# Attention partials summed and divided in the feed-forward stage, a third PSUM bank for turned quarters, and negated scores

## The chip, the cores and the metric

One Trainium2 chip, and one of its cores. The metric is the device time of one execution in microseconds (us); lower is better.

## The reference, cut to what matters

One transformer block over `x` of 2 batches, 2048 tokens and 512 features, with 16 heads of 32 features, in float32:

```python
q = (x @ Wq + bq)...; k = (x @ Wk + bk)...; v = (x @ Wv + bv)...     # x: layer norm, scaled and shifted
scores = jnp.einsum('bhqd,bhkd->bhqk', q / math.sqrt(HEAD_DIM), k) + attention_bias   # (2, 16, 2048, 2048)
scores = jnp.where(src_mask, -jnp.inf, scores)
probs = jax.nn.softmax(scores, axis=-1)
ctx = jnp.einsum('bhqk,bhkd->bhqd', probs, v)         # back to (2, 2048, 512)
x = x + (ctx @ Wo + bo)
h = _ln(x) * g2 + beta2
x = x + gelu2(h @ W1 + b1) @ W2 + b2                  # 2048 hidden features
# then pairs of features are rotated by theta and phi
```

The attention bias alone is 512 MB, and it is read once.

## The kernel before, in words

The kernel has three stages, one after the other: `phase_a` (layer norm, q, k and v, written to DRAM; the mask is turned into a bf16 penalty), `phase_b` (attention) and `phase_c` (output projection, feed-forward and rotation). Data go from stage to stage through DRAM scratch tensors.

**Stage B.** A tile is 128 queries of one head against all 2048 keys. There are 512 tiles, in 64 trips of 8 (`R = 8`). A trip is one head and 1024 queries; it has two units (`hh`) of 4 tiles. The tiles live in `ring`, which has 8 slots of 128x2048 float32, one for each `j` of a trip. Every engine runs its own list of steps, one step for each tile, and waits on semaphores that the others count up:

- SyncE loads the bias of a tile into its slot as soon as the tile that had the slot eight steps before has been turned (`sp.wait_ge(turned, ...)`). Behind the load of `j == 0` stand four loads of the next trip's keys, behind those of `j == 2` and `j == 6` four loads of queries. On the first of 16 trips of a group the penalty (`penb`, 512 KB a tile) is loaded too.
- GpSimd adds the penalty (L450).
- TensorE computes scores in two halves of 1024 (`score`, L601). VectorE adds each half to the slot and keeps a running maximum (`add`, L506), and then makes `neg_max` out of it (L520).
- ScalarE takes the exponential of a tile and its sum (L555).
- TensorE turns (transposes) the tile in four quarters of 512 through two PSUM banks (`turn`, L618). ScalarE copies quarters 0 and 1 to `probT` (L564), VectorE quarters 2 and 3 (`copy_quarter`, L492).
- TensorE multiplies with the values (`weigh`, L634), in four bands of 32 partitions, each of which holds a partial context. For each unit ScalarE copies the four bands out (`ctxp`, L571). TensorE adds them up with eight matmuls against `sel4` (`close`, L646), VectorE takes the reciprocal of the sums (L524) and multiplies by it (`ctx_out`, L532), and ScalarE stores 64 KB to `ctx_scratch`.

In a step `i` VectorE runs: add of half 0, add of half 1, `neg_max`, quarter 2 and quarter 3 of tile `i-2`. TensorE runs: scores of tile `i`, quarters 0 and 1 of tile `i-2`, `close` (at `j % 4 == 2`), `weigh`, quarters 2 and 3.

**Stage C.** 8 units of 512 tokens. The feed-forward of unit `u` (`ffn`) and the front of unit `u+1` (`front`: context turned, Wo, layer norm, turned) are interleaved in 18 steps `f` by the helper `supertiles`:

```python
for f in range(FB): front(0, f)
with eng.Fori(0, NU - 1) as u:
    for f in range(FB + 2):
        ffn(u, f)
        if f < FB:
            front(u + 1, f)
```

`ffn` at step `f` is, on TensorE, the up matmuls of block `f` (L944) and the down matmuls of block `f-2` (L954); on ScalarE the gate (L812); on VectorE `hidden` (L872). At step 17 VectorE adds the residual and rotates (L877 to L890), and GpSimd adds the two halves of the rotation (L781). `front` at steps 0 to 3 turns one quarter of the context of the next unit: TensorE transposes `ctx_in` (L916) and ScalarE copies it out to `ctxT` (L799). VectorE adds `bo` to `xm_in` at step 0 (L832).

Of the kernel before, what the change touches and what calls it, by code (L numbers as in the profile page):

```python
# [18 lines left out]
F32 = mybir.dt.float32  # L19
# [20 lines left out]
MASKED = -3.0e38  # L40
QSCALE = 1.0 / math.sqrt(DH)
# [24 lines left out]
def phase_a(nc, sem, x, timestep, mask, theta, phi, W_ada, b_ada, Wq, bq, Wk, bk, Wv, bv, freqs,  # L66
            q_parts, k_parts, v_heads, xm_scratch, pen_scratch, ident, sel4, trig):

    with ExitStack() as ctx:
# [76 lines left out]
        def _(pool):  # L146

            nc.gpsimd.memset(ident[:], 0.0).then_inc(const_ready, 1)
            nc.gpsimd.memset(sel4[:], 0.0).then_inc(const_ready, 1)
            pool.wait_ge(const_ready, 2)  # L150
            nc.gpsimd.affine_select(out=ident[:], in_=ident[:], compare_op=ALU.not_equal, fill=1.0,
                                    base=0, pattern=[[-1, P]], channel_multiplier=1).then_inc(const_ready, 1)
            for j in range(4):
                pool.wait_ge(const_ready, 3 + j)
                nc.gpsimd.affine_select(out=sel4[:], in_=sel4[:], compare_op=ALU.not_equal, fill=1.0,
                                        base=-DH * j, pattern=[[-1, DH]], channel_multiplier=1).then_inc(const_ready, 1)
# [159 lines left out]
        def _(pe):  # L316
# [11 lines left out]
            pe.wait_ge(const_ready, 7)  # L328
# [22 lines left out]
def phase_b(nc, sem, side, q_parts, k_parts, v_heads, pen_scratch, ctx_scratch, ident, sel4):  # L351
# [4 lines left out]
    R = 8  # L356
# [5 lines left out]
    TRIPS = GROUPS * H  # L362
    NT = TRIPS * R
    UNITS = TRIPS * 2
    assert R == 2 * QT and QR * P == N
    with ExitStack() as ctx:
# [9 lines left out]
        max_part = sb("max_part", [P, R, CH])  # L376
        neg_max = sb("neg_max", [P, R])
        sums = sb("sums", [P, R])
        recip = sb("recip", [P, 2, QT])
        ctxp = sb("ctxp", [P, TOK])  # L380
        ctx_out = sb("ctx_out", [P, 2, QT, DH])
        scores = [ctx.enter_context(nc.psum_tensor(f"scores{i}", [P, CW], F32)) for i in range(CH)]
        bankT = [ctx.enter_context(nc.psum_tensor(f"b_T{i}", [P, N], F32)) for i in range(2)]
        bank_ctx = ctx.enter_context(nc.psum_tensor("bank_ctx", [P, TOK], F32))
        bank_sum = ctx.enter_context(nc.psum_tensor("bank_sum", [P, TOK], F32))
# [9 lines left out]
        max_ready = sem("max_ready")  # L395
# [6 lines left out]
        ctx_summed = sem("ctx_summed")  # L402
        recip_ready = sem("recip_ready")
        ctx_normed = sem("ctx_normed")
        ctx_stored = [sem(f"ctx_stored{i}") for i in range(2)]
# [3 lines left out]
        block = ctx.enter_context(nc.Block())  # L409

        @block.sync
        def _(sp):
# [27 lines left out]
            for i in range(2):  # L440
                sp.wait_ge(ctx_stored[i], 16 + TRIPS * 16)
# [36 lines left out]

        @block.vector
        def _(dve):  # L480
            dve.sem_inc(ctx_normed, 1)

            def copy_quarter(it, j, n):

                t, k = it * R + j - 2, (j - 2) % R
# [523 lines left out]
```

## Time and profile before

| | |
|---|---|
| median of three runs | 3857.47 us (3857.29 to 3860.09) |
| the profiled execution | 3858.61 us |
| its span, first to last instruction | 3857.0 us |
| mean granted TensorE clock | 0.965 |
| busy: PE, DVE, ACT, POOL | 93%, 66%, 49%, 56% of the span |
| stage B, from the first GpSimd tile to the first load of stage C | 519.4 to 2721.4 us |
| stage C | 2721.4 us to the end |

The profiled execution takes 1.6 us more than its span. PE stands for TensorE matmuls, PEld for its weight loads, DVE for VectorE, ACT for ScalarE, POOL for GpSimd, SP for SyncE; SPq and ACTq are the DMA issues of these engines. Ends of matmuls are modelled and overlap, so that starts are the better guide to TensorE's pace.

### The profile page before, as it was taken

The page shows a single profiled execution, that of the slowest core. Times are in us where ns is not written, and L with a number is a line of the kernel's source. Part 1 is how long each engine was busy: PE and PEld are TensorE (multiplying, and loading weights), DVE is VectorE, ACT ScalarE, POOL GpSimd, SP SyncE. Part 2 cuts the span into 40 slices and gives each one's busy share as a digit, 9 for nine tenths or more (in the row PEclk, how much of TensorE's full clock was granted, in tenths as well). Part 3 has the DMA queues.
Part 4 walks back from the last instruction along what each step waited for, and adds up shares of the span by engine and source line. Part 5 has one row for each costly group of instructions (what it writes and reads, how often), then busy time and mean ns, then how long its engine had stood idle before and what let it go on. Part 6 is the DMA issues. An engine that isn't in the chain of part 4 may idle for free. (4 is left out here: it accounts for less than half of the span.)

```text
span 3857.0 us, 64984 instructions
## 1 busy us (share of the span) xinstructions
PE 3589.8 (93%) x18848; PEld 2074.9 (54%) x18848; DVE 2561.2 (66%) x4882; ACT 1899.6 (49%) x2483; POOL 2165.7 (56%) x595
## 2 busy tenths in 40 slices
PE   6778769999999999999999999999699999999997
PEld 2334336666666666666666666666344444444443
DVE  3444449999989999899999899999322323232232
ACT  1221227777777777777777777777211111111110
POOL 0000059999989999999999999999000000000000
PEclk8889879999999999999999999999799999999999
DMA  5556489999999999999999999997511101101000
GB/s 188 169 173 201 147 288 319 315 313 312 319 348 317 316 312 312 337 331 313 317 315 313 341 319 314 317 313 271 155 22 33 22 11 33 22 22 22 11 11 11
DMA packets 327444, 822.20 MB, mean 213 GB/s; under 512 B 165376, under 2 KB 181760, under 8 KB 250624
## 3 DMA queue, kind: packets, MB, share of 16 engines
q1 hardware_dynamic: 277376, 746.44, 57.6%
q10 hardware_dynamic: 45312, 58.74, 5.6%
q0 software_dynamic: 4736, 16.78, 1.2%
q8 instruction: 10, 0.16, 0.0%
q14 instruction: 10, 0.08, 0.0%
HBM read 737.95 MB, written 83.89 MB: 213 GB/s over the span
## 5 line engine op out<-in xcount | busy, mean ns | idle before, releaser
L450 POOL TENSOR_TENSOR ring<-ring,penb 128x2048 f32<-128x2048 f32 x512 | 2089.4, 4119 | 599.6 <-DMA penb<-pen_scratch 542.5
L555 ACT ACTIVATE ring<-ring,neg_max 128x2048 f32<-128x2048 f32 x512 | 1029.1, 2010 | 515.4 <-DVE neg_max L520 515.4
L618 PEld LDWEIGHTS b_T<-ident,ring 128*128 128x128 f32 x8192 | 886.7, 141 | 623.5 <-ACT probT L564 427.6
L618 PE MATMUL b_T<-ident,ring 128*128 128x128 f32 x8192 | 1158.7, 281 | 1.9 <-DVE probT L492 1.3
L492 DVE COPY probT<-b_T 128x512 f32<-128x512 f32 x1024 | 668.0, 684 | 70.5 <-PE b_T L618 70.5
L506 DVE CUSTOM_DVE_ANT_0 ring<-scores,ring,max_part 128x1024 f32<-128x1024 f32 x512 | 657.6, 1284 | 74.2
L506 DVE CUSTOM_DVE_ANT_0 ring<-scores,ring 128x1024 f32<-128x1024 f32 x512 | 622.2, 1215 | 43.6 <-PE scores L601 43.6
L601 PE MATMUL scores<-keys,queries 128*128 (+1 forms) x2048 | 606.5, 418 | 46.6 <-DMA queries<-q_parts 45.4
L781 POOL TENSOR_TENSOR y_out<-rot_a,rot_b 128x512 f32<-128x512 f32 x32 | 50.3, 1572 | 1020.8 <-DVE rot_b L890 1020.0
L564 ACT COPY probT<-b_T 128x512 f32<-128x512 f32 x1024 | 542.8, 580 | 30.2 <-PE b_T L618 24.0
L634 PE MATMUL bank_ctx<-probT,values 128*32 128x512 f32 x4096 | 546.8, 607 | 0.0
L944 PE MATMUL c_up<-hT,w 128*128 (+1 forms) x1024 | 478.3, 611 | 41.6 <-DVE hidden L872 40.7
L954 PE MATMUL c_acc<-w,hidden 128*128 128x512 f32 x1024 | 458.9, 592 | 0.0
L872 DVE SCALAR_TENSOR_TENSOR hidden<-c_up,b_col,gate 128x512 f32<-128x512 f32 x128 | 95.9, 750 | 519.1 <-ACT gate L812 517.7
L812 ACT ACTIVATE gate<-c_up,b_scaled 128x512 f32<-128x512 f32 x128 | 88.0, 687 | 673.2 <-PE c_up L944 673.0
L601 PEld LDWEIGHTS scores<-keys,queries 128*128 128x128 f32 x2048 | 349.3, 191 | 96.8 <-issue 45.7
L944 PEld LDWEIGHTS c_up<-hT,w 128*128 128x128 f32 x1024 | 197.2, 197 | 275.1 <-issue 232.1
L954 PEld LDWEIGHTS c_acc<-w,hidden 128*128 128x128 f32 x1024 | 194.0, 190 | 241.8 <-issue 241.5
L221 ACT ACTIVATE std<-mean_var,eps_a 128x4 f32<-128x4 f32 x8 | 2.4, 297 | 311.8 <-DVE mean_var L283 311.8
L837 DVE TENSOR_TENSOR x<-c_fore,xm_in 128x512 f32 (+1 forms) x32 | 22.1, 692 | 167.5 <-PE c_fore L925 167.5
L646 PE MATMUL bank_sum<-sel,ctxp 128*128 128x32 f32 x1024 | 125.1, 266 | 0.7 <-ACT ctxp L571 0.7
L646 PEld LDWEIGHTS bank_sum<-sel,ctxp 128*128 128x128 f32 x1024 | 124.4, 192 | 1.6 <-ACT ctxp L571 1.6
(91 smaller groups left out, 1926.1 us busy)
## 6 DMA issues: line engine op xcount, KB each, us to landing
ring<-in_fside_Bx16xSxS SPq DMA_DIRECT2D x512, 1024.0 KB, 5.8
keys<-k_parts SPq DMA_DIRECT2D x256, 256.0 KB, 6.8
values<-v_heads ACTq DMA_DIRECT2D x128, 256.0 KB, 6.0
queries<-q_parts SPq DMA_DIRECT2D x512, 64.0 KB, 6.8
pen_scratch<-pen SPq DMA_DIRECT2D x8, 2048.0 KB, 7.2
penb<-pen_scratch SPq DMA_DIRECT2D x32, 512.0 KB, 12.3
xin<-in_x ACTq DMA_DIRECT2D x8, 1024.0 KB, 5.2
mask_in<-in_mask_Bx1xSxS_bk ACTq DMA_DIRECT2D x8, 1024.0 KB, 7.3
```

The costliest lines, as they stand in the source:

```text
L450: nc.gpsimd.tensor_tensor(ring[:, j, :], ring[:, j, :], penb[:, j, :], ALU.add).then_inc(masked, 1)
L492: nc.vector.tensor_copy(probT[:, hh, QR * n:QR * (n + 1), q * P:(q + 1) * P], bankT[n - 2][:].rearrange("p (c q) -> p c q", c=QR)).then_in ...
L506: nc.vector.tensor_tensor_reduce(out=at, in0=scores[c][:], in1=at, scale=1.0, scalar=max_part[:, j, c - 1:c] if c else MASKED, op0=ALU.add ...
L555: nc.scalar.activation(ring[:, k, :], ring[:, k, :], ACT.Exp, bias=neg_max[:, k:k + 1], accum_out=sums[:, k:k + 1]).then_inc(exp_done, 1)
L564: nc.scalar.copy(probT[:, hh, QR * n:QR * (n + 1), q * P:(q + 1) * P], bankT[n][:].rearrange("p (c q) -> p c q", c=QR)).then_inc(out_act, 1)
L601: last = nc.tensor.matmul(scores[c][:, n * N:(n + 1) * N], queries[:, hh, q * P:(q + 1) * P], keys[:, bass.ds(it % 2, 1), c * CW + n * N:c ...
L618: last = nc.tensor.transpose(bankT[n % 2][:, c * P:(c + 1) * P], ring[:, slot, at:at + P], ident[:])
L634: last = nc.tensor.matmul(bank_ctx[DH * c:DH * (c + 1), :], values[:, hh, QR * n + c, :], probT[:, hh, QR * n + c, :], start=(n == 0), sto ...
L646: last = nc.tensor.matmul(bank_sum[:, t * DH:(t + 1) * DH], ctxp[:, t * P:(t + 1) * P], sel4[:], start=True, stop=True)
L872: nc.vector.scalar_tensor_tensor(out=hidden[:, f % 4, :], in0=up[f % 2][:], scalar=b1_col[:, f:f + 1], in1=gate[:, f % 2, :], op0=ALU.add, ...
L944: last = nc.tensor.matmul(up[f % 2][:], w1[:, c, f * P:(f + 1) * P], hT[:, bass.ds(u % 2, 1), c, :].rearrange("p o n -> p (o n)"), start=( ...
L954: last = nc.tensor.matmul(acc[t][:], hidden[:, k % 4, t * P:(t + 1) * P], w2[:, k, :], start=(k == 0), stop=(k == FB - 1))
```

## The change

- `close`, `sel4`, the bank `bank_sum`, the reciprocal and the multiplication leave stage B. ScalarE stores `ctxp` itself, all four bands, 256 KB a unit. It waits for the store of the unit before it copies again.
- The freed bank becomes a third bank for turned quarters. Waits that stood ahead of a group of matmuls now stand inside the group before (ahead of its last part). VectorE's copy of quarter 3 moves from the end of step `i` to between the two adds of step `i+1`.
- The adds write the negated score and keep a running minimum. That minimum is the bias of the exponential, so `neg_max` is gone. Minima and sums of all tiles are kept on chip for stage C (one copy of 128x8 a trip).
- In stage C the sixteen 256 KB loads of partial contexts of a unit (in four groups `c`, two buffers) replace four loads of 256 KB. VectorE takes the reciprocals and adds a term from the minima at step 0, spreads four heads' reciprocals over 32 columns each (`recip_wide`), and TensorE transposes these in place of the context. VectorE adds up the four bands (`tensor_reduce` over 4x512) and multiplies by the turned reciprocals. ScalarE no longer copies `ctxT`. `bo` is added at step 3.

```diff
         def turn_bank(t, n):
+            return bankT[(0, 1, 2, 0)[n] if t % 2 == 0 else (2, 1, 0, 2)[n]]
...
             def step(it, j):                                   # VectorE, stage B
                 add(it, j, 0)
+                keep_low(it, j)
+                copy_quarter(it, j, 3, 3)
                 add(it, j, 1)
-                if live(i, NT):
-                    dve.wait_ge(added, i * CH + CH)
-                    nc.vector.tensor_scalar(neg_max[:, j:j + 1], max_part[:, j, CH - 1:CH], -2.0, 0.5, ALU.mult, ALU.mult).then_inc(max_ready, 1)
-                copy_quarter(it, j, 2)
-                if dividing:
-                    dve.wait_ge(exp_done, i - 1)
-                    nc.vector.reciprocal(recip[:, hh, :], sums[:, hh * QT:(hh + 1) * QT]).then_inc(recip_ready, 1)
-                copy_quarter(it, j, 3)
-                if j % QT == 2: ...   nc.vector.tensor_tensor(ctx_out[:, hh, :, :], bank_sum..., recip..., ALU.mult)
+                copy_quarter(it, j, 2, 2)
...
+            def free_before_turn(it, j, c):                    # TensorE, ahead of the last matmul of a score half
+                t = it * R + j - 2
+                if live(t, NT):
+                    if c == 0:
+                        pe.wait_ge(exp_done, t + 1)
+                    else:
+                        need(pe, out_dve, t * 2 - 1)
...
+                for c in range(4):                             # weigh
+                    if c == 2 and live(t, NT):
+                        need(pe, out_dve, t * 2)
...
-                if j % QT == 2:
-                    close(it, j)
...
+                if j % QT == 1 and live(unit, UNITS):          # ScalarE
+                    act.wait_ge(pv_done, PV0 + unit + 1)
+                    act.wait_ge(ctx_stored, unit * 16 + 16)
+                    nc.scalar.copy(ctxp[:], bank_ctx[:]).then_inc(ctx_copied, 1)
...
             def load(v):                                       # SyncE, stage C
+                for c in range(DB):
+                    if isinstance(v, int) and c == 2:
+                        load_vectors()
+                    need(sp, parts_used, v * DB + c - 1)
+                    for k in range(4):
+                        sp.dma_start(parts[DH * k:DH * (k + 1), c % 2, :, :],
+                                     ctx_scratch[bass.ds(v * H + 4 * c + k, 1)].rearrange("o (g d) q -> d (o g) q", d=DH)).then_inc(part_ld[c % 2], 16)
...
                 if f == 0:                                     # VectorE, stage C, front(v, f)
+                    nc.vector.tensor_scalar(undefined[:], in_unit(low_all, v), 2.0, 0.0, ALU.mult, ALU.mult)
+                    link(nc.vector.reciprocal(recip[:], in_unit(sums_all, v)), 1)
+                    link(nc.vector.tensor_tensor(recip[:], recip[:], undefined[:], ALU.add), 2)
+                    need(dve, wo_done, v * QT)
+                if f < DB:
+                    need(dve, recip_turned, v * DB + f - 1)
+                    nc.vector.tensor_copy(recip_wide[:, f % 2]..., recip[:, 4 * f:4 * f + 4, :]...to_broadcast([P, QT, 4, DH])).then_inc(wide_ready, 1)
+                    dve.wait_ge(part_ld[f % 2], v * 128 + (f // 2) * 64 + 64)
+                    nc.vector.tensor_reduce(ctxT[:, f, :], parts[:, f % 2].rearrange("p g q -> p q g"), AXIS_X, ALU.add).then_inc(parts_used, 1)
+                    dve.wait_ge(parts_used, v * DB + f + 1)
+                    dve.wait_ge(recip_turned, v * DB + f + 1)
+                    nc.vector.tensor_tensor(ctxT[:, f, :], fore[f % 2][:], ctxT[:, f, :], ALU.mult).then_inc(ctxT_ready, 1)
...
                 if f < DB:                                     # TensorE, stage C, front(v, f)
-                    if f == 0:
-                        pe.wait_ge(ctx_ld, v * 64 + 64)
+                    pe.wait_ge(wide_ready, v * DB + f + 1)
...
                     for t in range(QT):
-                        last = nc.tensor.transpose(fore[f % 2][:, t * P:(t + 1) * P], ctx_in[:, t, 4 * f:4 * f + 4, :]...)
+                        last = nc.tensor.transpose(fore[f % 2][:, t * P:(t + 1) * P], recip_wide[:, f % 2, t, :], ident[:])
```

## Rows read from the trace of the kernel before

**Rows 1.** Busy time by engine in stretches of stage B
```profile
core 0: us, PE busy (x) PEld busy (x) DVE busy (x) ACT busy (x) POOL busy (x), PEclk, DMA share, GB/s
519.37:2692.20 2172.83, 2139.97 (x15172) 1406.35 (x15173) 1986.12 (x3806) 1636.77 (x2155) 2089.43 (x512) 0.99 0.93 319
1073.09:1110.04 36.95, 34.56 (x241) 22.88 (x240) 31.11 (x60) 25.82 (x35) 32.82 (x9) 0.95 1.03 376
...
1817.27:1850.55 33.28, 33.28 (x239) 21.68 (x238) 30.90 (x61) 25.41 (x35) 32.64 (x9) 1.00 0.94 317
```

**Rows 2.** Timeline of GpSimd alone: start, us, what, [idle before and its releaser]
```profile
1073.09 4.10 POOL L450 TENSOR_TENSOR ring<-ring,penb 128x2048 f32<-128x2048 f32 x1 [5.19 <-DMA penb<-pen_scratch]
...
1110.04 130.53 POOL L450 TENSOR_TENSOR ring<-ring,penb 128x2048 f32<-128x2048 f32 x32 [2.37 <-DMA ring<-in_fside_Bx16xSxS]
...
2018.65 32.68 POOL L450 TENSOR_TENSOR ring<-ring,penb 128x2048 f32<-128x2048 f32 x8 [0.74 <-DMA ring<-in_fside_Bx16xSxS]
```

**Rows 3.** Timeline of stage B, VectorE: a closing step, then a plain one
```profile
2036.09 1.22 DVE L506 CUSTOM_DVE_ANT_0 ring<-scores,ring 128x1024 f32<-128x1024 f32 x1
...
2039.41 1.29 DVE L492 COPY probT<-b_T 128x512 f32<-128x512 f32 x2 [0.48 <-PE b_T L618]
...
2040.62 0.28 DVE L532 TENSOR_TENSOR ctx_out<-bank_sum,recip 128x128 f32<-128x128 f32 x1
...
2040.82 1.22 DVE L506 CUSTOM_DVE_ANT_0 ring<-scores,ring 128x1024 f32<-128x1024 f32 x1
...
2044.82 1.22 DVE L506 CUSTOM_DVE_ANT_0 ring<-scores,ring 128x1024 f32<-128x1024 f32 x1
...
2046.19 1.28 DVE L506 CUSTOM_DVE_ANT_0 ring<-scores,ring,max_part 128x1024 f32<-128x1024 f32 x1
...
2047.52 0.15 DVE L520 TENSOR_SCALAR neg_max<-max_part 128x1 f32<-128x1 f32 x1
2047.62 1.29 DVE L492 COPY probT<-b_T 128x512 f32<-128x512 f32 x2
...
2048.83 1.22 DVE L506 CUSTOM_DVE_ANT_0 ring<-scores,ring 128x1024 f32<-128x1024 f32 x1
```

**Rows 4.** The same timeline: slot `j == 1` turned, loaded and taken
```profile
2042.45 1.09 PE L618 MATMUL b_T<-ident,ring 128*128 128x128 f32 x8
...
2043.72 4.45 SPq L419 DMA_DIRECT2D ring<-in_fside_Bx16xSxS  x2
...
2052.41 4.10 POOL L450 TENSOR_TENSOR ring<-ring,penb 128x2048 f32<-128x2048 f32 x1 [1.07 <-DMA ring<-in_fside_Bx16xSxS]
```

**Rows 5.** Timeline where stage B ends: the first load of stage C
```profile
2721.43 0.41 SPq L760 DMA_DIRECT2D wo<-in_L_cond_Wo  x1
```

**Rows 6.** Timeline of stage C between units 1 and 2
```profile
3053.05 0.73 DVE L872 SCALAR_TENSOR_TENSOR hidden<-c_up,b_col,gate 128x512 f32<-128x512 f32 x1
...
3053.71 3.40 DVE L832 TENSOR_TENSOR xm_in<-xm_in,bo_all 128x512 f32<-128x512 f32 x4
...
3053.83 6.51 PE L944 MATMUL c_up<-hT,w 128*128 x8 [5.75 <-DVE hidden L872]
...
3060.19 3.60 PE L954 MATMUL c_acc<-w,hidden 128*128 128x512 f32 x8
...
3061.19 0.75 DVE L872 SCALAR_TENSOR_TENSOR hidden<-c_up,b_col,gate 128x512 f32<-128x512 f32 x1 [3.13 <-ACT gate L812]
```

**Rows 7.** Waits in stage C: in total, times, longest
```profile
PE c_up L944 <- DVE hidden L872: 40.7, 7, 6.6
```

**Rows 8.** TensorE's timeline around two stops in stage B
```profile
2163.33 1.19 PE L601 MATMUL scores<-keys,queries 128*128 x4 [2.03 <-DMA queries<-q_parts]
...
2199.23 1.96 PE L601 MATMUL scores<-keys,queries 128*128 x4 [2.55 <-DMA queries<-q_parts]
```

**Rows 9.** Busy time in a short stretch behind the stop of rows 6
```profile
3055.00:3057.00 2.00, 2.00 (x4) 0.86 (x3) 2.00 (x4) 0.00 (x0) 0.56 (x1) 0.50 0.25 94
```

**Rows 10.** Timeline of the first unit's front in stage C
```profile
2733.60 0.49 SPq L764 DMA_DIRECT2D b_col<-in_L_cond_b  x1
...
2740.75 2.50 DVE L832 TENSOR_TENSOR xm_in<-xm_in,bo_all 128x512 f32<-128x512 f32 x4 [0.25 <-DVE b_scaled L899]
...
2743.82 16.52 PE L925 MATMUL c_fore<-wo,ctxT 128*128 128x512 f32 x32 [0.67 <-ACT ctxT L799]
```

More of the change, by code:

```diff
@@ L148, in _ @@
             nc.gpsimd.memset(ident[:], 0.0).then_inc(const_ready, 1)
-            nc.gpsimd.memset(sel4[:], 0.0).then_inc(const_ready, 1)
-            pool.wait_ge(const_ready, 2)
+            pool.wait_ge(const_ready, 1)
             nc.gpsimd.affine_select(out=ident[:], in_=ident[:], compare_op=ALU.not_equal, fill=1.0,
                                     base=0, pattern=[[-1, P]], channel_multiplier=1).then_inc(const_ready, 1)
[L153 to L156, printed above, removed]
         @block.sync
@@ L439, in _ @@
                         load_head(b, pair, h, False)
-            for i in range(2):
-                sp.wait_ge(ctx_stored[i], 16 + TRIPS * 16)
+            sp.wait_ge(ctx_stored, UNITS * 16 + 16)
         @block.gpsimd
@@ L511, in step, with keep_low @@
+            def keep_low(it, j):
+                if j == 0 and (not known(it) or it > 0):
+                    dve.wait_ge(added, it * R * CH)
+                    nc.vector.tensor_copy(low_all[:, bass.ds(it - 1, 1), :].rearrange("p o n -> p (o n)"), low[:]).then_inc(low_kept, 1)
             def step(it, j):
-                i = it * R + j
-                unit, hh = closing(it, j) + 1, 1 if j < QT else 0
-                dividing = j % QT == 1 and live(unit, UNITS)
                 add(it, j, 0)
+                keep_low(it, j)
+                copy_quarter(it, j, 3, 3)
@@ L621, in weigh @@
-            def weigh(it, j):
-                n = (j - 2) % QT
-                unit = it * 2 - 2 if j < 2 else it * 2 - 1 if j < 6 else it * 2
-                hh = 1 if 2 <= j < 6 else 0
-                if live(unit, UNITS):
-                    if n == 0:
-                        pe.wait_ge(v_in[hh], it * 16 if j == 2 else it * 16 + 16)
-                        need(pe, ctx_copied, unit)
-                    pe.wait_ge(out_act if n < 2 else out_dve, (unit * QT + QT - 1) * 2 + n % 2 + 1)
-                    for c in range(4):
+                for c in range(QR):
+                    if c == 2:
+                        if n == 0 and live(t, NT):
+                            need(pe, out_act, t * 2)
+                        if n == 1:
+                            copied_before_weigh(it, j)
+                        if n == 2 and live(t, NT):
+                            pe.wait_ge(out_act, t * 2 + 1)
+                    if live(t, NT):
+                        at = (QR * n + c) * P
+                        last = nc.tensor.transpose(turn_bank(slot, n)[:, c * P:(c + 1) * P], ring[:, slot, at:at + P], ident[:])
@@ L634, in weigh @@
                         last = nc.tensor.matmul(bank_ctx[DH * c:DH * (c + 1), :], values[:, hh, QR * n + c, :],
                                                 probT[:, hh, QR * n + c, :], start=(n == 0), stop=(n == 3))
-                    if n == 3:
-                        last.then_inc(pv_done, 1)
-            def close(it, j):
-                unit = closing(it, j)
-                if live(unit, UNITS):
-                    pe.wait_ge(ctx_copied, unit + 1)
-                    pe.wait_ge(ctx_normed, unit + 1)
-                    for t in range(QT):
-                        last = nc.tensor.matmul(bank_sum[:, t * DH:(t + 1) * DH], ctxp[:, t * P:(t + 1) * P], sel4[:],
-                                                start=True, stop=True)
-                    last.then_inc(ctx_summed, 1)
+                if live(unit, UNITS) and n == 3:
+                    last.then_inc(pv_done, 1)
```

191 lines of the change are left out of this document (93 added, 98 removed).

## The prediction

> **What bounds the kernel now.** I read the page first. It says 93% for TensorE, but that is a mean over stages, so I went on to busy time by stretches. In stage B [rows 1] three engines stand near full: GpSimd is busy 2089.4 of 2172.8 us, VectorE 1986.1, and TensorE looks full because modelled ends overlap. The DMA engines have a share of 0.93 at 319 GB/s. The reader should not stop at "GpSimd 96%". The timeline of GpSimd alone shows when it stops: it runs eight tiles in 32.68 us (4.085 each) and then waits 0.5 to 1.5 us, always for the load of slot `j == 1` [rows 2]. Who is late there? The load of that slot was issued at 2043.72, just after the slot's old tile had been turned (the turn starts at 2042.45 and takes 1.09), and it landed 8.7 us later, when GpSimd had stood idle for 1.07 us [rows 4]. So GpSimd is held by slots that come free late, and they come free late because VectorE lags behind it.
>
> VectorE's steps tell the pace: a plain step takes 4.01 us from add to add (2044.82 to 2048.83), without a gap worth naming; the closing step takes 4.73 (2036.09 to 2040.82), with 0.48 us of waiting for TensorE, which had the `close` matmuls in its queue, and 0.2 us for `ctx_out` [rows 3]. There are two closing steps in a trip: 6 x 4.03 + 2 x 4.73 = 33.6 us, and that is the period of GpSimd's stops (33.3 us in one trip [rows 1]). Behind a stop for the penalty, when VectorE has caught up, GpSimd runs 32 tiles without any stop (130.53 us, 4.08 each) [rows 2]. That is what the loop can do when VectorE isn't late. So stage B is bound by VectorE's list with TensorE's `close` in it, and GpSimd's own 32.68 us per trip is a floor 0.9 us below.
>
> In stage C TensorE has its work back to back (3.43 us for each group of eight) but for one stop between units: 5.75 us, while VectorE rotates the unit that has ended. TensorE then resumes at a low clock, so that the group takes 6.36 us (3053.83 to 3060.19) [rows 6]; the granted clock there is 0.50, which is 1.2 GHz [rows 9]. There are seven such stops, 40.7 us in sum [rows 7].
>
> **Stage B, what is removed.** From VectorE's plain step: `neg_max` and its wait, 0.10 us (from 2047.52 to 2047.62), and with quarter 3 between the adds the second add no longer waits for the first one's accumulator. That gap was 0.15 us (1.22 of work in a pitch of 1.37 up to 2046.19). 4.01 becomes about 3.8. From the closing step go the waiting, the reciprocal and `ctx_out` as well (0.7 us). The one new copy of 128x8 costs what `neg_max` does, 0.15 us a trip. Sum for VectorE: 8 x 3.8 + 0.3 = 30.7 us a trip, 2 us under GpSimd. TensorE loses `close`. The new order ties a chain together: quarter 3 copied, half of `weigh`, two turns, half a score, add, quarter 3 copied again. With 0.5 + 1.1 + 0.6 + 1.3 + 0.6 us it is about 4.0, just below 4.085. So I take GpSimd as the new bound. The lower bound of the gain is that this chain, or the DMA, takes the trip to 33.2 us.
>
> The slot's cycle gets slack: once VectorE runs right behind GpSimd, a tile is turned some 11 us after GpSimd has done with it (add, quarter, add 3.3; exponential 2.2; one more step 4.1; turns 1.4), not about 21 us (taken at 2018.65 [rows 2], turned at 2043.54 [rows 4], less 4.1), so a load has some 17 us where it had 8.3. The loads of a trip are 10.6 MB, and the stores of whole `ctxp` add 0.39 MB: 11.0 MB in 32.7 us is 337 GB/s. The trace has moved 376 GB/s for 37 us [rows 1]. It is close (0.94 at 317 makes 1.00 at 337, against 1.03 shown), so I leave some stops standing.
>
> Idle time of GpSimd in stage B is 2172.8 - 2089.4 = 83.4 us. About 10 us of it belong to the first nine tiles, which are bound by the first loads, some 9.7 to each of three later loads of the penalty, the rest (about 45) to the 0.9 us stops. I leave 8 for the start, 3 for each penalty load (more slack in front of them) and 0.15 a trip: 25 us. Gain 58. Bounds: 10 us left (gain 73), or half of it left (gain 42; 25 if the chain binds).
>
> **The end of stage B.** From GpSimd's last tile (2692.2) to the first load of stage C (2721.4) [rows 5] it is 29.2 us, because VectorE was two tiles behind. With no lag I count 3.3 (adds) + 2.2 (exponential) + 4 (turns and copies) + 3.6 (four `weigh`) + 5 (copy, store) = 18: gain 11 (bounds 6 and 13).
> Stage B in sum: -69 us (-35 to -86).
>
> **Stage C, between units.** Here is the cost. TensorE's transposes at steps 0 and 1 used to need only loaded data. Now they wait for `recip_wide`, which VectorE makes *after* `hidden` of the same step, in the order of `supertiles`. At a unit's start VectorE is still rotating. Before, TensorE did up(0), the transposes, up(1), the transposes, and only stopped ahead of up(2). Let R be the start of `hidden`(0), 3053.05. Before: up(2) starts at R + 0.78 and is done at R + 7.1 [rows 6].
> After: `hidden` 0.75; three small operations, two of them with a wait (0.15 each by `neg_max`, more for 64 elements and waits: 0.7); the wide copy (half of 1.29 for two quarters [rows 3], or a quarter of 2.50 [rows 10]: 0.6); and 0.5 for GpSimd's presence. The transposes start at R + 2.55. TensorE has stood longer, so its clock is low for the 5.9 us that the group's 6.36 in place of 3.43 implies (2.93 us lost at half speed): transposes 0.9, then 5.0 us give 2.5 of up(1)'s 3.43, and 0.93 is left: up(1) is done at R + 9.4. Gate and `hidden`(1) end 1.75 us behind the end of an up (3060.19 to 3061.94) [rows 6], wide copy 0.6: R + 11.7. Transposes 0.45, up(2) 3.43: R + 15.6. That is 8.5 us later than before.
> TensorE's second stop is then about 2.35 us. What becomes of the clock? After a stop of 2.03 us the scores ran at full pace (1.19 us), after 2.55 us they took 1.96 [rows 8]. So it lies between; a fall costs from 0.8 us here [rows 8] to 2.9 [rows 6]. I charge 1.1: 9.6 us. It happens in six of the seven stops (the last unit has no front behind it): 58 us. Bounds: 6 x 7.5 = 45, and 6 x 11.5 = 69.
> The 0.5 for GpSimd rests on the addition of `bo`, which took 3.40 us beside GpSimd's `y_out` [rows 6] and 2.50 without [rows 10]. By the Trainium skill (SBUF — State Buffer, "SBUF: two separate sides") a VectorE operation in a two-port mode and a GpSimd operation lock each other out for a whole instruction; the copy to `recip_wide` would then wait its full turn, 0.9 instead of 0.5, 2.4 us more in the sum. This doesn't enter it.
>
> **Stage C, the rest.** In the first pass of the loop no rotation stands before it, but up(0), wait 3.05 (1.75 + 0.7 + 0.6), up(1), wait 2.35 are new: 5.4 us, and 3.5 for the clock: 9 (5 to 12).
> The first front is serial. Before, Wo starts at 2743.8; the last small vector was issued at 2733.6 and landed at 2740 [rows 10]. After: cheaper issues put the vectors 5 us earlier (2735.5), then VectorE alone does small operations 0.7 and four times wide copy 0.6, band sum 2.4 (2048 elements; four additions of 128x512 take 2.50), multiplication 0.7, and waits for the loads of groups 2 and 3, which start only when a buffer is free: 2752.5. That is +9 (4 to 16; a band sum at half pace, for its stride of 512 elements, would add 8).
> At steps 2 to 15 nothing is late: `hidden`, wide copy, band sum, multiplication and `bo` together are 6.9 us in a TensorE step of 7.3, and the wide copy is done 2.4 us behind up, under the 3.43 of down. Less work on ScalarE is worth nothing; it waits anyway. `sel4` in stage A is worth nothing.
> Stage C in sum: 58 + 9 + 9 = +76 us (+54 to +97).
>
> **Sum.** 3858.6 (the profiled execution: span 3857.0 and 1.6 around it) - 69 + 76 = 3865.6. The runs' median is 1.1 us below the profiled one, so I say 3865.
>
> **Rivals.**
> *GpSimd never stops (faster).* The slack of 17 us hides every load; idle falls to 10 us, and with the tail the gain is 84 to 86; the second stops leave the clock up (as after 2.03 us [rows 8]), so stage C costs 69. Time 3843. For it: 130 us without a stop [rows 2]. Against: DMA share 1.00. It decides where stage B gains over 84 us, or 8 us more than C costs.
> *Stage B stays bound (slower).* The chain through half a `weigh`, or the DMA at 337 GB/s, keeps the trip at 33.2 us or more: stage B gives 35, the time is 3900. For it: my chain is only 0.1 us under GpSimd's pace. Against: the 32 tiles at 4.08.
> *The band sum is slow (slower).* Twice 2.4 us: +8 in the first front, +3 where `bo` shares step 3 with it in seven units: about 3885.
> *The boundary costs nothing (faster)*, since VectorE's new work hides behind TensorE's: then 3797. Against it stands the order of the two queues; I give it almost nothing.
>
> **How the numbers follow.** A measurement here can tell about 0.2% (7.7 us) from no change. My forecast, 0.43, with its own range 3852 to 3880: 0.05 faster, 0.19 same, 0.19 slower. GpSimd never stops, 0.26: 0.22 faster, 0.04 same. Stage B stays bound, 0.20: slower. Band sum, 0.09: 0.02 same, 0.07 slower. Boundary free, 0.02: faster. Together: faster 0.29, same 0.25, slower 0.46. The range for 8 in 10 is 3836 to 3900.
>
> **What would show it.** Right: VectorE's add-to-add step equals GpSimd's 4.09, GpSimd's stops for the ring are gone, and its last tile ends near 2634; `close` gone; TensorE stops twice at a unit's start, before both groups of transposes, the first some 11 us long, and the unit takes 9 to 10 us more than its 135. Wrong: steps of VectorE at 4.15 or more with TensorE waiting inside `weigh`; or ring loads that take over 15 us; or units in stage C as long as before.

## The result, and the profile after

The kernel after takes 4272.76 us (median of 4 runs, 4261.22 to 4305.09) and the kernel before, on the same chip, 3857.91 us. The ratio is 1.109, with a 95% interval of 1.103 to 1.115. The prediction said 3865 us, with a range of 3836 to 3900. It is 408 us short.

The profiled execution has a span of 4268.9 us. The end of stage B is found by the first load of stage C, as in [rows 5]; timeline of the kernel after, where stage C begins:

```profile
3054.45 0.40 SPq L774 DMA_DIRECT2D wo<-in_L_cond_Wo  x1
```

| | before | after | difference | predicted |
|---|---|---|---|---|
| up to the first GpSimd tile | 519.4 | 516.6 | -2.7 | 0 |
| stage B | 2202.1 | 2537.8 | +335.7 | -69 |
| stage C, to the span's end | 1135.6 | 1214.5 | +78.9 | +76 |

Stage C came out near its sum. Nearly the whole error is in stage B. Busy time of the kernel after, from the first GpSimd tile to 18 us before the end of stage B, and in 800 us from its middle:

```profile
core 0: us, PE busy (x) PEld busy (x) DVE busy (x) ACT busy (x) POOL busy (x), PEclk, DMA share, GB/s
516.64:3036.00 2519.36, 2410.91 (x14230) 1394.32 (x14231) 1996.97 (x3124) 1675.98 (x2165) 2089.39 (x512) 0.98 0.87 285
...
1600.00:2400.00 800.00, 770.41 (x4551) 445.12 (x4551) 638.54 (x994) 534.15 (x691) 661.26 (x163) 0.99 0.86 284
```

The same 800 us of the kernel before:

```profile
1600.00:2400.00 800.00, 792.25 (x5643) 521.29 (x5642) 735.30 (x1411) 606.75 (x800) 766.42 (x189) 1.00 0.94 323
```

VectorE is busy 639 us in these 800 (735 before) and GpSimd 661 (766 before); the DMA moves less, 284 GB/s instead of 323; the granted clock is 0.99. TensorE's 770 us look full, but they hold the modelled ends that overlap, and the waits below show it standing still. When every engine has idle time and the DMA moves less than it did before, look for a chain of waits that sets the pace. The waits of the kernel after (us in total, times, longest):

```profile
PEld bank_ctx L641 <- DVE probT L489: 451.4, 503, 4.7
POOL ring L443 <- DMA ring<-in_fside_Bx16xSxS: 380.0, 209, 5.8
DVE ring L505 <- PE scores L587: 210.8, 436, 27.2
...
PE scores L587 <- DMA queries<-q_parts: 34.3, 5, 26.5
```

The wait *inside* `weigh` occurs in nearly every step (503 of 512). One step on the timeline of the kernel after:

```profile
2010.73 1.91 PE L641 MATMUL bank_ctx<-probT,values 128*32 128x512 f32 x8
2010.84 0.08 DVE L505 DVE_READ_ACCUMULATOR2_ANT low_part<- 128x1 f32 x1
2010.84 0.69 DVE L489 COPY probT<-b_T 128x512 f32<-128x512 f32 x1
...
2011.58 0.14 PEld L641 LDWEIGHTS bank_ctx<-probT,values 128*32 128x32 f32 x4 [0.71 <-DVE probT L489]
...
2012.56 1.09 PE L615 MATMUL b_T<-ident,ring 128*128 128x128 f32 x8
...
2013.41 1.18 PE L587 MATMUL scores<-keys,queries 128*128 x4
...
2014.36 1.22 DVE L505 CUSTOM_DVE_ANT_0 ring<-scores,ring 128x1024 f32<-128x1024 f32 x1 [0.41 <-POOL ring L443]
...
2015.39 1.05 PE L641 MATMUL bank_ctx<-probT,values 128*32 128x512 f32 x4
2015.51 0.08 DVE L505 DVE_READ_ACCUMULATOR2_ANT low_part<- 128x1 f32 x1
2015.51 2.79 DVE L514 COPY low_all<-low 128x8 f32 x1
2018.22 0.68 DVE L489 COPY probT<-b_T 128x512 f32<-128x512 f32 x1
...
2018.95 1.05 PE L641 MATMUL bank_ctx<-probT,values 128*32 128x512 f32 x4 [2.50 <-DVE probT L489]
```

Two things are to be seen. The first is the chain that the prediction named, at another length. From start to start, quarter 3's copy takes 0.61 us, the semaphore 0.13, the second half of `weigh` 0.98, the two turns 0.85, the scores until the add 0.95, the add until the copy 1.15: 4.67 us, which is the distance from one `weigh` to the next (2010.73 to 2015.39). It is no accident of this step: 434 of the 511 distances from one tile's first add to the next lie within 0.01 us of 4.67. (The row at 2014.36 names GpSimd as the releaser. That isn't the wait: GpSimd had finished the tile of this add at 2002.83. The add waited for its scores.) The second is the copy of the minima, 128x8 elements, for which the prediction had 0.15 us. Here it takes 2.79 us, and it stands in the middle of the chain; TensorE waits 2.50 us for what is behind it. One trip is 8 x 4.67 + 1.59 = 39.0 us (1.59 is the mean of all 64 copies), where the prediction had 32.8. Over 64 trips the difference is 392 us. The error of stage B is 335.7 + 69 = 404.7 us, and the other 13 are its end. GpSimd's last tile there:

```profile
3019.06 4.10 POOL L443 TENSOR_TENSOR ring<-ring,penb 128x2048 f32<-128x2048 f32 x1 [1.81 <-DMA ring<-in_fside_Bx16xSxS]
```

From its end (3023.16) to the first load of stage C (3054.45) it is 31.3 us. It was 29.2 before, and the prediction had 18.

Why is such a small copy slow? All 64 of them, in the kernel after (min, median and max in ns):

```profile
L514 DVE COPY low_all<-low x64: 161/1454/4081, 570.2 to 3040.6; 128x8 f32 x63, 128x8 f32<-128x8 f32 x1
```

And GpSimd alone around the one above:

```profile
2006.06 24.41 POOL L443 TENSOR_TENSOR ring<-ring,penb 128x2048 f32<-128x2048 f32 x6 [3.23 <-DMA ring<-in_fside_Bx16xSxS]
```

GpSimd's tiles end at 2006.06 + 4.07 n. The third ends at 2018.27; the copy ends at 2018.30. It waited until GpSimd had finished the tile it was at. So it is with the others: 55 of the 64 copies end 0.03 us after the end of a GpSimd tile, the other nine took 0.16 to 0.17 us, and no copy took longer than one tile (4.08 us). The Trainium skill says so (SBUF — State Buffer, "SBUF: two separate sides"): a VectorE operation in a two-port mode and a GpSimd operation exclude each other for a whole instruction. This trace agrees, with 0.16 to 4.08 us for one and the same copy; that this copy ran in such a mode is not shown by the trace itself. The other copies of VectorE in the loop, all 1024 of them, read PSUM and took 0.68 to 0.69 us.

Stage C of the kernel after, VectorE and TensorE between units, answers to [rows 6]:

```profile
3279.27 0.74 DVE L893 SCALAR_TENSOR_TENSOR hidden<-c_up,b_col,gate 128x512 f32<-128x512 f32 x1
3279.93 0.82 DVE L837 TENSOR_SCALAR undefined<-low_all 128x64 f32 x1
3280.67 0.54 DVE L838 RECIPROCAL recip<-sums_all 128x64 f32 x1
...
3281.69 0.43 DVE L843 COPY recip_wide<-recip 128x512 f32<-128x512 f32 x1 [0.22 <-DVE recip L839]
3282.03 3.65 DVE L846 TENSOR_REDUCE ctxT<-parts 128x512 f32<-128x2048 f32 x1
```

```profile
3282.25 1.11 PE L936 MATMUL c_fore<-ident,recip_wide 128*128 128x128 f32 x4 [11.16 <-DVE recip_wide L843]
3283.16 5.59 PE L964 MATMUL c_up<-hT,w 128*128 x8
3290.73 0.66 PE L936 MATMUL c_fore<-ident,recip_wide 128*128 128x128 f32 x4 [1.98 <-DVE recip_wide L843]
3291.22 3.60 PE L964 MATMUL c_up<-hT,w 128*128 x8
...
3426.53 1.11 PE L936 MATMUL c_fore<-ident,recip_wide 128*128 128x128 f32 x4 [12.34 <-DVE recip_wide L843]
```

TensorE stops twice at a unit's start, 11 us and then 2 us, as described ahead. The group behind the first stop takes 5.59 us (granted clock 0.65 between 3283 and 3289), the one behind the second 3.60 (granted clock 1.00). The unit takes 144.3 us (3282.25 to 3426.53). Before, it was 136.0 us from 3053.83 [rows 6] to the same stop of the next unit:

```profile
3189.78 5.11 PE L944 MATMUL c_up<-hT,w 128*128 x8 [5.75 <-DVE hidden L872]
```

Over the six such periods of each kernel the mean is 143.5 us after and 135.3 before, 8.2 more. The first front, which answers to [rows 10]:

```profile
3074.06 0.17 DVE L920 TENSOR_SCALAR b_scaled<-b_col 128x16 f32<-128x16 f32 x1 [18.96 <-DMA b_col<-in_L_cond_b]
3074.49 0.20 DVE L837 TENSOR_SCALAR undefined<-low_all 128x64 f32<-128x64 f32 x1 [0.25 <-DVE b_scaled L920]
...
3091.34 3.63 DVE L846 TENSOR_REDUCE ctxT<-parts 128x512 f32<-128x2048 f32 x1 [0.22 <-DMA parts<-ctx_scratch]
...
3095.75 15.81 PE L945 MATMUL c_fore<-wo,ctxT 128*128 128x512 f32 x32 [3.46 <-DVE ctxT L849]
```

Wo starts 41.3 us after the first load (3054.45), where it took 22.4. `undefined` takes 0.20 us here, where GpSimd adds nothing, and 0.82 us between units (3279.93), where it ends 0.06 us after GpSimd's addition for `y_out` (3279.44 to 3280.69).

### The profile page after: what moved, and what is told of

Its sections match the earlier page's. It is cut to its first block and busy times, and to the rows that moved or that the text cites. A ratio compares the mean times of both kernels' runs of the same rounds, so it can differ in the third digit from the quotient of the medians.

```text
span 4268.9 us, 61552 instructions
## 1 busy us (share of the span) xinstructions
PE 3850.7 (90%) x17824; PEld 2054.2 (48%) x17824; DVE 2718.7 (64%) x4298; ACT 1913.9 (45%) x2451; POOL 2162.8 (51%) x590
## 5 line engine op out<-in xcount | busy, mean ns | idle before, releaser
L541 ACT ACTIVATE ring<-ring,low 128x2048 f32<-128x2048 f32 x512 | 1028.3, 2008 | 611.5 <-DVE low L505 592.0
L615 PEld LDWEIGHTS b_T<-ident,ring 128*128 128x128 f32 x8192 | 928.4, 142 | 485.0 <-issue 436.2
L615 PE MATMUL b_T<-ident,ring 128*128 128x128 f32 x8192 | 1101.6, 278 | 2.3 <-DVE probT L489 2.3
L641 PE MATMUL bank_ctx<-probT,values 128*32 128x512 f32 x4096 | 985.9, 608 | 84.3 <-DVE probT L489 84.1
L489 DVE COPY probT<-b_T 128x512 f32<-128x512 f32 x1024 | 704.4, 688 | 298.8 <-PE b_T L615 298.8
L505 DVE CUSTOM_DVE_ANT_0 ring<-scores,ring,low_part 128x1024 f32<-128x1024 f32 x512 | 652.3, 1274 | 0.5 <-PE scores L587 0.2
L587 PE MATMUL scores<-keys,queries 128*128 (+1 forms) x2048 | 614.3, 422 | 35.4 <-DMA queries<-q_parts 34.3
L641 PEld LDWEIGHTS bank_ctx<-probT,values 128*32 128x32 f32 x4096 | 147.4, 108 | 538.7 <-DVE probT L489 451.4
L557 ACT COPY ctxp<-bank_ctx 128x512 f32<-128x512 f32 x128 | 75.0, 586 | 164.4 <-PE bank_ctx L641 160.0
L936 PE MATMUL c_fore<-ident,recip_wide 128*128 128x128 f32 x128 | 25.2, 331 | 128.4 <-DVE recip_wide L843 128.4
```

The lines of the kernel that those rows point to most:

```text
L489: nc.vector.tensor_copy(probT[:, hh, QR * n:QR * (n + 1), q * P:(q + 1) * P], turn_bank(k, n)[:].rearrange("p (c q) -> p c q", c=QR)).then ...
L505: nc.vector.tensor_tensor_reduce(out=at, in0=scores[c][:], in1=at, scale=-1.0, scalar=low_part[:, j:j + 1] if c else -MASKED, op0=ALU.add, ...
L541: nc.scalar.activation(ring[:, k, :], ring[:, k, :], ACT.Exp, bias=low[:, k:k + 1], scale=-1.0, accum_out=column(sums_all, trip, k)).then_ ...
L587: last = nc.tensor.matmul(scores[c][:, n * N:(n + 1) * N], queries[:, hh, q * P:(q + 1) * P], keys[:, bass.ds(it % 2, 1), c * CW + n * N:c ...
L615: last = nc.tensor.transpose(turn_bank(slot, n)[:, c * P:(c + 1) * P], ring[:, slot, at:at + P], ident[:])
L641: last = nc.tensor.matmul(bank_ctx[DH * c:DH * (c + 1), :], values[:, hh, QR * n + c, :], probT[:, hh, QR * n + c, :], start=(n == 0), sto ...
```

## The experiments

Theory A of the first four runs is the reading above: two costs in the chain, the parted `weigh` and the locked copy. The rivals were the DMA queue and the order of VectorE's list. Stage B is always counted from the first GpSimd tile to the first load of stage C; where a run was timed once, it says so. The length of a stage comes from one profile. The kernel after and e11 have the same stage B, and their profiles give 2537.8 and 2558.3 us; a difference of 20 us between two profiles therefore shows little.

### e1: the wait moved out of `weigh`

```diff
 for c in range(4):
-    if c == 2 and live(t, NT):
-        need(pe, out_dve, t * 2)
     ...
+if live(t, NT):
+    need(pe, out_dve, t * 2)
```

> The wait for VectorE's copy of quarter 3 moves from the middle of the four band matmuls of weigh to behind them, ahead of quarter 2. Theory (a chain through half a weigh): the step of 4.67 us is quarter copied, second pair of bands 0.98, two turns 0.83, scores until the add starts 0.97, add 1.15, quarter 0.61; without the pair of bands it is 3.7, under GpSimd's 4.085, so stage B falls from 2538 us to 2150-2200 and the whole to 3880-3930 us. Rival (the larger stores and the DMA at its limit hold the ring loads, 380 us of GpSimd's waiting stand before them): no change, 4270. Rival (the order of VectorE's list): no change either.

Measured: 4136.7 us (4120.5 to 4163.9), ratio 1.074 [1.071, 1.078]; stage B 2386.7. TensorE's timeline of e1:

```profile
2009.70 1.06 PE L639 MATMUL bank_ctx<-probT,values 128*32 128x512 f32 x8
...
2010.70 1.09 PE L615 MATMUL b_T<-ident,ring 128*128 128x128 f32 x8
```

The eight instructions of `weigh` take 1.00 us from their start to the next group's; the four bands run side by side. In the kernel after they took 1.83 us (2010.73 to 2012.56). Steps are down to 3.83 and 3.96 us. That part of the theory held. The forecast of the time did not (4136.7 us for 3880 to 3930, stage B 2386.7 for 2150 to 2200): only 151 us of stage B went, while another wait grew, TensorE for the queries, from 34.3 us to 211.3, in 61 waits, about one in a trip.

### e2: a wait in the middle that is always met

As e1, with the wait inside `weigh` kept for the tile before (`t * 2 - 1`), which has always been met by then. It tells apart whether the wait instruction parts the bands or the waiting.

> As the first, but a wait that is always met stays in the middle of the four band matmuls. If it is the unmet wait that parts the bands, this one is as fast as the first (3880-3930 us). If any wait there parts them, weigh keeps its 1.84 us against 0.99 and TensorE's own list is 4.67 us a step: about 4200-4270 us.

Measured, once: 4152.73 us; stage B 2417.6, near e1's; the whole lies between the two forecasts, and the group itself tells. TensorE's timeline of e2:

```profile
2003.82 1.07 PE L641 MATMUL bank_ctx<-probT,values 128*32 128x512 f32 x8
...
2004.81 1.09 PE L615 MATMUL b_T<-ident,ring 128*128 128x128 f32 x8
```

0.99 us again, so a wait that is met costs this group nothing. In the kernel after the wait wasn't met, and the second pair of bands then took 0.98 us by itself, behind 0.85 for the first.

### e3: no copy of the minima

`keep_low` is left out and `low_all` set to zero once. The term that makes rows without any key undefined is thus left out of the result.

> Leaves out the copy of the minima (128x8, once a trip) and sets them to zero once, so that the term for rows without any key in the last stage is always zero. The copy took 0.16 to 4.08 us, mean 1.75. Theory (VectorE's copy inside SBUF is locked out while GpSimd works on a tile, and it stands in the chain): 64 x 1.6 = 100 us less, 4170 us. Rival (the slack of the slots hides it): no change, 4270 us.

Measured, once: 4155.08 us; stage B 2424.7, 113 less than after. The 64 copies took 102 us in sum (64 x 1.59), so the copy costs about what it takes; the 11 us between are within what two profiles differ by.

### e4: both

> Both: wait behind weigh, and no copy of the minima (set to zero once, the term for rows without any key is zero). If the chain and the copy are all that went wrong in stage B, it runs at GpSimd's pace, about 2130 us, and the whole takes what I predicted, 3850-3880 us. If the DMA is at its limit it stays above 3900.

Measured: 4043.76 us (4024.5 to 4066.4), ratio 1.049 [1.044, 1.054]; stage B 2304.4. Both costs of the chain are gone, and stage B is still 102 us longer than before. Waits and timeline of e4:

```profile
PE scores L585 <- DMA queries<-q_parts: 229.4, 63, 26.5
POOL ring L443 <- DMA ring<-in_fside_Bx16xSxS: 161.5, 91, 4.4
```

```profile
1994.13 1.77 SPq L426 DMA_DIRECT2D queries<-q_parts  x4
...
1997.35 16.60 SPq L413 DMA_DIRECT2D ring<-in_fside_Bx16xSxS  x4
...
1999.36 0.36 ACTq L561 DMA_DIRECT2D ctx_scratch<-ctxp  x1
...
2008.05 2.07 PE L585 MATMUL scores<-keys,queries 128*128 x4 [3.08 <-DMA queries<-q_parts]
```

The queries were issued at 1994.13 and TensorE got them 14 us later. It then worked at the lower clock (scores 2.07 us instead of 1.18; granted clock 0.50 between 2008 and 2010); the mean granted clock of e4 is 0.942. The forecast (3850 to 3880 us, if the chain and the copy were all) failed, so my first theory was incomplete. Two rivals for the rest: the 256 KB stores (0.39 MB more in a trip), which share the DMA with the queries, or the place at which the queries are issued.

The trace says which queries are late. Those for the first unit of a trip are issued after four 256 KB loads of keys, and landed 13.6 us after their issue (from the first of the four issues to the last landing, median over the trips); those for the second unit have no keys before them and landed after 6.0 us. TensorE used the former 14.0 us after their issue, as soon as they were there.

### e5 and e6: smaller stores, or earlier queries

e5 is e4 with only 128 of the 512 columns of `ctxp` stored, 64 KB as before; stage C loads them four times, so its result isn't the context. e6 is e4 with one line changed:

```diff
-                    if qt == 2:
+                    if qt == 1:
                         sp.wait_ge(scored, ...)        # four loads of queries
```

> The kernel with the wait behind weigh and no copy of the minima, and it stores only the first 128 of 512 columns of the partial contexts (64 KB a unit, as before the change; the last stage loads these four times, and its result is not the context). To be read for stage B alone, which took 2304 us there. Theory A (the DMA is at its limit: 11.4 MB a trip moved at the 323 GB/s that the kernel before reached too): stage B falls by 3.5%, to 2225 us. Theory B (latency: queries land late because they are issued behind the load of slot 2, and TensorE stops 3.6 us a trip for them): stage B stays within 20 us of 2304.

> The same kernel (wait behind weigh, no copy of the minima) with full stores, and the loads of queries issued behind the load of slot 1 and 5 instead of 2 and 6, one step earlier. Theory B: the 229 us that TensorE waited for queries go, stage B 2304 to some 2150 us, the whole 3890. Theory A: the waits for queries turn into waits for the ring, stage B stays above 2270 us, the whole above 4000.

Measured: e5, once, 3896.56 us with stage B 2153.6; e6 3914.12 us (3898.0 to 3921.9), ratio 1.014 [1.011, 1.017], stage B 2175.7. Alone they give 151 and 129 us. For e5 both forecasts failed: theory A had 2225 us, theory B about 2304. e6 came near theory B (2150 and 3890), but not by its account, since more than half of the waits for queries stayed. Their waits, e5 first:

```profile
PE scores L585 <- DMA queries<-q_parts: 114.9, 42, 26.6
...
POOL ring L443 <- DMA ring<-in_fside_Bx16xSxS: 30.3, 24, 2.8
```

```profile
PE scores L585 <- DMA queries<-q_parts: 122.3, 49, 23.0
...
POOL ring L443 <- DMA ring<-in_fside_Bx16xSxS: 39.4, 34, 4.1
```

e6 moves 337 GB/s between 1600 and 2400 (DMA share 1.01), e4 324 (0.97). So e4 was not stopped by the rate alone. The reading that fits is that a small load, which TensorE needs at once, landed late behind large ones, and that each stop then made the slots late too. That the larger stores are harmless doesn't follow: a trip moves 11.3 MB by the sizes and counts of its transfers, which at GpSimd's pace of 32.7 us would be 345 GB/s, and no run reached that.

### e10: both of these together

> The kernel after with four edits together: wait of weigh moved behind it, no copy of the minima, only 128 of the 512 columns of ctxp stored (stage C loads them four times, so its result is not the context), queries issued one tile earlier. Small stores alone took stage B from 2304 to 2154 us, early queries alone to 2176. Theory A (both relieve one and the same lateness, a query load behind a full DMA queue): together they stop at GpSimd's pace, stage B 2125 to 2150 us. Theory B (two separate losses that add up): 2025 us, which GpSimd's 2089 us of work excludes; so if they were separate, stage B would be at its floor of about 2115 us.

Measured, once: 3874.57 us; stage B 2124.5, with 55.6 us of waits for queries. That is 29 us under e5 and 51 under e6. The run doesn't decide between the theories: 2124.5 lies at the edge of the first (2125 to 2150) and near the floor that the second would meet (2115). It shows the floor: VectorE's add starts 0.14 us behind the end of GpSimd's tile in more than half of the steps.

### e7: the kernel before with the negated scores alone

```diff
-  ... scale=1.0,  scalar=max_part... if c else MASKED,  op0=ALU.add, op1=ALU.max, ...
+  ... scale=-1.0, scalar=max_part... if c else -MASKED, op0=ALU.add, op1=ALU.min, ...
-  nc.vector.tensor_scalar(neg_max[:, j:j + 1], ...).then_inc(max_ready, 1)
-  act.wait_ge(max_ready, i)
-  ... ACT.Exp, bias=neg_max[:, k:k + 1],
+  act.wait_ge(added, i * CH)
+  ... ACT.Exp, bias=max_part[:, k, CH - 1:CH], scale=-1.0,
```

`close`, the two banks, the order of the steps and stage C are those of before. Rows without any key are not made undefined.

> The kernel before with the negated scores alone: no operation for the negated maximum, its exponential's bias is the running minimum; closing, banks, order and the last stage as before (the term for rows without any key is left out). VectorE's step falls by 0.10 to 0.15 us. If stage B is bound by VectorE's list, 512 x 0.1 to 0.15 = 50 us less at most, down to GpSimd's pace: 3810-3830 us. If the DMA bounds it already, nothing: 3858.

Measured: **3794.04 us** (3785.4 to 3809.2), ratio 0.984 [0.982, 0.986]; stage B 2130.4, 72 less than before. The direction was as forecast, the size larger (3810 to 3830 had been expected). VectorE and GpSimd of e7:

```profile
2012.35 1.22 DVE L506 CUSTOM_DVE_ANT_0 ring<-scores,ring 128x1024 f32<-128x1024 f32 x1
...
2016.13 1.22 DVE L506 CUSTOM_DVE_ANT_0 ring<-scores,ring 128x1024 f32<-128x1024 f32 x1
```

```profile
1618.11 522.30 POOL L450 TENSOR_TENSOR ring<-ring,penb 128x2048 f32<-128x2048 f32 x128 [2.12 <-DMA ring<-in_fside_Bx16xSxS]
```

The plain step falls from 4.01 us [rows 3] to 3.78, by 0.23 and not by 0.10 to 0.15, and GpSimd runs 128 tiles without a stop, 4.08 each, where it stopped once in a trip before [rows 2]. This confirms what bounded stage B before: VectorE's list, with a floor of GpSimd just below. One part of the change is enough to get there.

### e9: e7 with early queries

> The kernel before with two edits: the negated scores (as in the run that made them alone, 3794.0 us) and the loads of queries issued behind the tile of j == 1 in place of j == 2. With the negated scores alone TensorE waited 50.4 us for queries in sum, in 15 waits, and GpSimd 11.2 us for tiles. Theory A (VectorE's list bounded stage B, and with it gone GpSimd's own pace does): GpSimd already runs without stops, so earlier queries give nothing, 3785 to 3800 us. Theory B (late queries hold the loop wherever VectorE doesn't): the 50 us of waits go and the time falls by 15 us or more, under 3780.

Measured: **3778.46 us** (3776.0 to 3779.9), ratio 0.979 [0.977, 0.980]; stage B 2121.0, waits for queries 38.9 us in 6. The median is 15.6 us under e7's, which is just what theory B asked. But the profiles show less: stage B 9.4 us shorter, 11.5 us less of waiting for queries, 5.4 less of GpSimd's for tiles. The profile of e7 is that of its fastest run (3785.43), and e7 and e9 ran on different chips, e7 with a wider spread. That e9 is faster is shown (the ranges do not touch), that earlier queries give 15 us is not. This is the fastest version found, 81 us under the kernel before on its chip; like e7 it lacks the term for rows without keys.

### e8: the kernel after, repaired

The whole result of the reference, with five edits: e1's wait, the minima copied by ScalarE in place of VectorE, early queries, the reciprocals and the first two spread copies made one unit ahead, two additions in place of the `tensor_reduce`.

> The change repaired: wait behind weigh, minima copied by ScalarE, queries one step earlier, reciprocals of quarters 0 and 1 spread one unit ahead (before VectorE's rotation), and the four bands added by two additions in place of the reduction. The last stage should lose its 8.5 us a unit and most of the first front's extra: from 1214 us back to 1150. With theory B stage B takes 2150 and the whole 3820; with theory A it is 2290 and 3960.

Measured: 3853.38 us (3838 to 3864), ratio 0.998 [0.996, 0.999]; stage B 2184.0, stage C 1152. 419 us are back, which is all that the change cost, and it is no faster than before by anything that matters. Stage C came out as forecast (1150), stage B between the two theories (2150 and 2290). Queries are still waited for (140.3 us in 58).

### e11: only the order in stage C

```diff
+ def ahead(v): ...          # undefined, reciprocal, spread copies of quarters 0 and 1 of unit v
  for f in range(FB + 2):
      ffn(u, f)
      if f < FB:
          front(u + 1, f)
+     if f == FB:
+         ahead(u + 2)
```

> The kernel after with one edit in stage C: the reciprocals and the spread copies of quarters 0 and 1 of the next unit are made one unit ahead, at step 16, so that TensorE's first two groups of transposes in a unit wait for nothing new. Theory A (the second stop per unit, caused by the order hidden, reciprocals, spread copy on VectorE, costs 8 us in each of six boundaries): the unit falls from 143.8 to about 135 us, stage C from 1214.5 to about 1155. Theory B (the band sum and the sixteen loads hold the unit): the unit stays above 140 us and stage C above 1195. Stage B is untouched and differs by chance alone.

Measured: 4242.38 us (4207.15 to 4254.12), ratio 1.097 [1.092, 1.102]; stage C 1163.9, 50.6 less than after. (The whole time fell by 30 us only, since stage B, the same in both, took 20.5 us more in this profile.) TensorE at two units' starts in e11:

```profile
3296.09 6.71 PE L982 MATMUL c_up<-hT,w 128*128 x8 [5.39 <-DVE hidden L911]
...
3432.57 6.74 PE L982 MATMUL c_up<-hT,w 128*128 x8 [5.76 <-DVE hidden L911]
```

One stop in place of two, and 136.5 us for a unit in place of 144.3. The order hidden, reciprocals, spread copy was the cost of the boundary: of the 8.2 us, 1.2 are left (the mean of six periods is 136.4 us, of the kernel before 135.3). That much at most is the band sum and the sixteen loads; in e8, which has two additions in place of the `tensor_reduce`, the mean is 135.4.

## Why the prediction was wrong, by its own steps

- **What bounds the kernel now: right.** VectorE's list, 0.9 us per trip above GpSimd: e7 shortened the list alone and met GpSimd's pace.
- **VectorE's list after: right in its sum, and beside the point.** VectorE was busy 1997 us in 64 trips, 31.2 a trip for 30.7, under GpSimd's 32.7. The list was no longer what bound.
- **The step that failed: "with 0.5 + 1.1 + 0.6 + 1.3 + 0.6 us it is about 4.0".** The mechanism was named and its size was wrong. Half of `weigh` was taken as half of its time, 0.5; it is 0.98 with 0.13 for the semaphore, since the four bands run at once, and two bands take as long as four. The half score was 0.95, not 0.6, counted from the start of the scores to the start of the add. The turns (0.85) and the add (1.15) were a little less. 4.67 in place of 4.1 (the terms as written add up to 4.1, already over GpSimd's 4.085; I rounded them in favour of the change). Eight steps make 37.4 us a trip, 4.5 over the 32.8 expected: 290 us in stage B. This price is read from the timeline; taking the wait out alone gave back 151 us (e1), because the queries then became late. The prediction's own sign of being wrong came true: "steps of VectorE at 4.15 or more with TensorE waiting inside `weigh`".
- **The second that failed: "the one new copy of 128x8 costs what `neg_max` does, 0.15 us".** It measured 1.59 us on average, all of it in the chain: 102 us. The third is the end of stage B, 31.3 us in place of 18, another 13: the lag that was to go had grown, for VectorE's first add of the last tile started 13.3 us behind GpSimd's end (10.3 before). The three make 405 us, and 404.7 were missing. The rule of the Trainium skill was weighed for `recip_wide` in stage C, where it would have been worth 2.4 us (it took 0.43 us between units and was not held up), and not for the copy in the loop where GpSimd works all the time. `neg_max` was the wrong row to price it by: with one element in a partition it took 153 to 156 ns in all of its 512 times before and was never held up. No run here shows why.
- **The rival "stage B stays bound" was the right one, with a price far too small.** Its chain was given 33.2 us a trip because that is the period before. Nothing in the trace bounded it there: a chain that is not bound by the list has its own period, and it was 39.0.
- **The DMA: right that 337 GB/s can be moved** (e6 does), **wrong in that the total alone decides, and in the total.** The 11.0 MB a trip leave out what was stored before and some of the loads; it is 11.3. And once the chain is cured, four 64 KB loads that arrive late cost 3 us a trip (e4). This was hidden in the kernel after, and would have been the next wait.
- **Stage C: right in the mechanism, and +78.9 against +76 is partly luck.** Six boundaries at 8.2 us are 49 (58 predicted; TensorE's second stop was 1.98 us and the clock stayed up behind it, 3.60 us for the group, so the 1.1 us charged for it was not due). The first front costs more, +18.9 in place of +9, for two reasons. The band sum took 3.63 us where 2.4 was put, four times: 5 us. And the last small vector was no earlier: `b_scaled`, which waits for it, starts 19.6 us after the first load of stage C (18.9 before [rows 10]), where the prediction had 14. The first pass of the loop took 9.7 us more (138.5 for 128.8), 9 predicted. The errors of the boundaries and of the first front cancel.
- **The third rival, the slow band sum,** was half true: 3.63 us lies midway between its 4.8 and the 2.4 of the forecast. Its time was also summed wrongly: 3865 and 8 and seven times 3 are 3894, and with 3 taken once 3876, not 3885.

What stays open: e5 and e7 both store 64 KB and issue the queries late, and yet e5 waits 114.9 us for them and e7 50.4. Both use the queries of a trip's first unit 11.3 to 11.7 us after their issue; they landed after 11.3 us in e5 and after 9.0 in e7. What makes them land later there was not tried. Nor was the third bank alone: none of these runs shows that it gains anything.

## What to carry to other kernels

Before a step is moved, lay the new chain end to end through every engine with measured start-to-start times, and sum it without rounding: a chain that runs through several engines once per tile costs its excess with every tile, however idle the engines are. Don't price half of a group of matmuls at half of its time: here the four bands of `weigh` took 0.99 us together and 1.83 with an unmet wait in their middle. And don't price a small VectorE copy from SBUF to SBUF beside a busy GpSimd by its size: here it took 1.59 us on average, some 0.4 of a GpSimd tile.

## What the runs showed of the hardware

- The bands: 8 instructions of `weigh` take 0.99 to 1.00 us (e2, e1), and 0.85 + 0.98 us when an unmet wait parts them (after). With a wait between them that is always met it is 0.99 us too (e2).
- The same 128x8 copy took 0.16 to 4.08 us beside GpSimd's tiles of 4.08 us, and 55 of 64 times it ended 0.03 us after a tile (after).
- The median time of a 1 MB bias load from issue to landing was 6.9 us in the kernel after, 10.5 in e4 and 11.9 in e6, of a 64 KB query load 5.4, 8.5 and 10.6: a load a sixteenth of the size landed only a little sooner. The rate doesn't tell this time: e7 moves 331 GB/s in the same 800 us, and its medians are 7.0 and 7.3 us.
- `tensor_reduce` over four bands with a stride of 512 elements took 3.62 to 3.70 us for 128x2048 elements of float32 in the kernel after, 1.8 ns for each of the 2048 columns.
